# Which rows SP and ACT fetch, and when: a four-part graph network on one core

## The chip, the cores and the metric

The kernel runs on one core of a Trainium2 chip. Times are device microseconds (us) of whole executions. The engines named below are TensorE (PE), VectorE (DVE), ScalarE (ACT), GpSimd (POOL) and SyncE (SP); each has its own instruction stream, and they meet only through semaphores. SP, ACT and POOL issue DMAs. A gather with row numbers in memory (an indirect DMA) is issued by POOL; SP and ACT issue plain transfers, whose address may come from a register.

## The reference

12,500 nodes with 64 features, 200,000 edges sorted by target node (`dst`). Four graph layers follow each other; each normalises x, applies relu and adds its result to x.

```python
h = relu(layernorm(x)); x = x + L0(h)   # attention: k, q, v per node type, 4 heads, weights per edge type
h = relu(layernorm(x)); x = x + L1(h)   # gated: edge score, softmax per target, max and mean of neighbours
h = relu(layernorm(x)); x = x + L2(h)   # polynomial of edge weights, from sum(h) of one end
h = relu(layernorm(x)); x = x + L3(h)   # three convolutions over edges:
# conv(h, W, b): m = concat(h[dst], h[src], edge_attr) @ W + b; segment_sum(m, dst)
# segment softmax, sum and max run over the edges with the same dst
```

What costs most is `h[src]`, one table row per edge, in five places: attention, gated, and three convolutions.

## The kernel before

**Layout.** The sorted edges are cut into 128 runs, one per partition, of J = 1564 edges. A step handles C = 23 edge columns of all partitions; NC = 68 steps make a pass. Sums over equal targets are running scans along the columns; a carry from partition to partition is mended afterwards through a "fixed row".

**Sequence.** `first_phase` (tables), `attention_edges_phase` (pass 1), `carry_phase`, `attention_end_phase`, `gated_edges_phase` (pass 2), `carry_phase`, `gated_end_phase`, and `conv_layer` three times (passes 3 to 5). Each phase opens a block of its own, in which every engine gets its list of instructions; at a block's end all engines drain and meet in a barrier. After `first_phase`, `attention_end_phase`, `gated_end_phase` and each `conv_layer` stands `clear_semaphores` (line 203): a block of its own in which SP clears the layer's semaphores, one instruction each (line 210).

**Gathering the source rows.** In `gather_columns` (line 905) POOL issues, for step c and each of its columns, one indirect DMA of 128 rows (line 912) into buffer c % ring, and before a step it waits until that buffer has been used (`ring` is 3 in attention and gated, 2 in conv). An *aided* step (`aided`, line 875) has one column less: its last column is brought by 128 one-row transfers in `fetch_rows` (line 889), in chunks of 16 rows, each with one load of 16 byte offsets into registers (line 896) and 16 transfers (line 901). `ATT_SHARE = (2, 5)` makes 25 of the first 64 steps aided in attention and gated, `CONV_SHARE = (3, 4)` makes 48 aided in each conv layer.

**Who fetches, and when.** In attention and gated SP fetches all 128 rows, half of them one iteration earlier than the other half. In conv SP fetches 80 and ACT 48, all for step c+2 in iteration c, once the copy of step c (`s_in`) has freed the buffer. These stand in order with SP's other work: in attention a load of q rows, then rows, then the wait for ACT's copy (`s_copied`) of the step before and its store; in gated rows, the wait for this step's copy, its store (line 1518); in conv the edge attributes (layer 0 alone, line 2125), some rows, the store (line 2148), the remaining rows.

**A gated step** (lines 1561 to 1615): DVE waits for the gathered rows and, if the step is aided, for the one-row transfers; it starts with line 1571, multiplies the rows by the exponentials at line 1603 (which signals `s_wtd`: the buffer is free), and scans. ACT then copies the results to the store buffer (to line 1539) and SP stores them. An attention step is alike: line 1055 is the first that uses gathered rows, ACT's exponentials begin at line 1006, and line 985 stores the last step (983 the others). In a conv step ACT copies the gathered rows (line 2190), DVE scans (line 2334), ACT copies the result (line 2195), SP stores it.

Of the kernel before, what the change touches and what calls it, by code (L numbers as in the profile page):

```python
# [28 lines left out]
P = 128  # L29
N = 12500  # L30
E = 200000
D = 64
H = 4
# [48 lines left out]
ATT_SHARE = (2, 5)  # L82
CONV_SHARE = (3, 4)
SP_ROWS = 80
# [200 lines left out]
def first_phase(nc, ctx, g, a):  # L285
# [3 lines left out]
    s_listed = sem("listed")  # L289
# [89 lines left out]
    with ExitStack() as inner:  # L379
# [8 lines left out]
        block = inner.enter_context(nc.Block())  # L388
# [277 lines left out]
        def _(dve):  # L666
# [205 lines left out]
            v.tensor_copy(g.a2row[:, :], ps_w[:, 260:260 + D])  # L872
# [55 lines left out]
def attention_edges_phase(nc, ctx, g):  # L928
# [27 lines left out]
    with nc.psum_tensor("ae_keep", [P, HF * C1], F32) as keep, nc.psum_tensor("ae_work", [P, HF * C1], F32) as work, \  # L956
            nc.psum_tensor("ae_prob", [P, C, H], F32) as prob_t, nc.Block() as block:
# [3 lines left out]

        @block.gpsimd
        def _(pool):

            pool.indirect_dma_start(out=mix[:, :, :].rearrange("p f j -> p (f j)")[:, 0:D], out_offset=None, in_=g.q_tab,
                                    in_offset=bass.IndirectOffsetOnAxis(ap=g.first[:, 0:1].bitcast(U32), axis=0))\
# [4 lines left out]
        def _(sp):  # L971
            for c in range(NC):
                wait(sp, s_qt, c)
                sp.dma_start(qin, q_rows[:, c * C:c * C + C, :]).then_inc(s_qin, 16)
                for later in (0, 1):
                    if aided(c + later, ATT_SHARE):
                        wait(sp, s_wtd, c + later - 2)
                        chunks = range(0, P // LOADS // 2) if later else range(P // LOADS // 2 if c else 0, P // LOADS)
                        fetch_rows(nc, sp, mybir.EngineType.SP, g.lists[:, 0, :], g.tab0, c + later, chunks,
                                   kvr[(c + later) % 3], s_side[side_of(c + later, ATT_SHARE)[0]])  # L980
# [8 lines left out]
        def _(act):  # L989
            def take(c):  # L990
# [28 lines left out]
        def _(dve):  # L1019
            v = nc.vector  # L1020
# [199 lines left out]
def attention_end_phase(nc, ctx, g, agg):  # L1220
# [34 lines left out]
    with ExitStack() as inner:  # L1255
# [4 lines left out]
        block = inner.enter_context(nc.Block())  # L1260
# [173 lines left out]


# [28 lines left out]
def gated_edges_phase(nc, ctx, g):  # L1464
# [26 lines left out]
    with nc.psum_tensor("ge_pen", [P, HF * C1], F32) as pen_flat, nc.psum_tensor("ge_decay", [P, HF * C1], F32) as decay_flat, \  # L1491
            nc.psum_tensor("ge_small", [P, 2, C], F32) as few, nc.Block() as block:  # L1492
# [4 lines left out]

        @block.gpsimd
        def _(pool):
            pool.indirect_dma_start(out=fv, out_offset=None, in_=g.s_tab,  # L1500
                                    in_offset=bass.IndirectOffsetOnAxis(ap=g.first[:, 0:1].bitcast(U32), axis=0))\
                .then_inc(s_first, 16)
            gather_columns(pool, g.tab1, g.src, rin, s_gath, s_wtd, ATT_SHARE)

        @block.sync
        def _(sp):
            sp.wait_ge(g.s_scattered, 16 * T)
            sp.dma_start(g.spread[:, :], g.s_start[0:EP, :].rearrange("(p j) a -> p (j a)", p=P)).then_inc(s_sin, 16)
            for c in range(NC):
                for later in (1, 2) if c else (0, 1, 2):  # L1510
                    if aided(c + later, ATT_SHARE):
                        wait(sp, s_wtd, c + later - 2)
                        half = P // LOADS // 2
                        chunks = range(0, half) if later == 2 else range(half if c else 0, 2 * half)
                        fetch_rows(nc, sp, mybir.EngineType.SP, g.lists[:, 1, :], g.tab1, c + later, chunks,
                                   rin[(c + later) % 3], s_side[side_of(c + later, ATT_SHARE)[0]])
                wait(sp, s_copied, c + 1)
                sp.dma_start(dest[:, c * C:c * C + C, 0:R1], out).then_inc(s_st, 16)
# [3 lines left out]
        def _(act):  # L1522
            act.wait_ge(s_init, 1)
            for c in range(NC):
# [8 lines left out]
                nc.scalar.activation(wts, args[:, 1, 1:C1], ACT.Exp).then_inc(s_den, 1)  # L1533

# [7 lines left out]
        def _(dve):  # L1542
            v = nc.vector
# [14 lines left out]
            for c in range(NC):  # L1558
# [7 lines left out]
                dve.wait_ge(s_gath[c % 3], gathered(c, ATT_SHARE, 3))  # L1566
                if aided(c, ATT_SHARE):
                    slot, full = side_of(c, ATT_SHARE)
# [473 lines left out]
def conv_layer(nc, ctx, g, a, k, out_rows):  # L2042
# [9 lines left out]
    s_gath = [pool_sem(g, f"gathered{b}") for b in range(2)]  # L2052
    s_side = [sem(f"side{n}") for n in range(4)]
    s_row = pool_sem(g, "fixed_rows")
# [10 lines left out]
    rin, ea, hd = ([None] * 2 for _ in range(3))  # L2065
    for b in range(2):
# [21 lines left out]
    with ExitStack() as inner:  # L2088
# [7 lines left out]
        def side_rows(eng, engine, c, chunks):  # L2096

            if aided(c, CONV_SHARE):
                fetch_rows(nc, eng, engine, g.lists[:, 2, :], g.tab3, c, chunks, rin[c % 2],
                           s_side[side_of(c, CONV_SHARE)[0]])  # L2100

        @block.gpsimd
        def _(pool):
            gather_columns(pool, g.tab3, g.src, rin, s_gath, s_in, CONV_SHARE)
# [16 lines left out]
        def _(sp):  # L2121
# [17 lines left out]
            early, late = range(0, SP_ROWS // LOADS // 2), range(SP_ROWS // LOADS // 2, SP_ROWS // LOADS)  # L2139
            for c in range(2):  # L2140
                side_rows(sp, mybir.EngineType.SP, c, range(0, SP_ROWS // LOADS))
# [32 lines left out]
        def _(act):  # L2174
            def take(c):
# [7 lines left out]
                act.wait_ge(s_gath[b], gathered(c, CONV_SHARE, 2))  # L2183
                if aided(c, CONV_SHARE):
                    slot, full = side_of(c, CONV_SHARE)
# [4 lines left out]
                nc.scalar.copy(chain[:, 0:D, 1:C1], rin[b].rearrange("p j f -> p f j")).then_inc(s_in, 1)  # L2190
# [25 lines left out]
            of_act = range(SP_ROWS // LOADS, P // LOADS)  # L2216
            scale(0)
            for c in range(2):
                side_rows(act, mybir.EngineType.Activation, c, of_act)
            for c in range(NC):  # L2220
# [10 lines left out]
                if len(of_act):  # L2231
                    act.wait_ge(s_in, c + 1)
                    side_rows(act, mybir.EngineType.Activation, c + 2, of_act)
# [129 lines left out]
def graph_layers(nc, a, out):  # L2363
    with ExitStack() as whole:
# [3 lines left out]
        with ExitStack() as ctx:  # L2368
            first_phase(nc, ctx, g, a)
            clear_semaphores(nc)  # L2370
        with ExitStack() as ctx:
            last = attention_edges_phase(nc, ctx, g)[:, C - 1, :]
# [4 lines left out]
            attention_end_phase(nc, ctx, g, agg)  # L2377
            clear_semaphores(nc)
        with ExitStack() as ctx:
            last = gated_edges_phase(nc, ctx, g)[:, C - 1, :]  # L2380
# [31 lines left out]
```

## Time and profile before

| | us |
|---|---|
| median of 3 runs (11754.08 to 11767.4) | 11756.29 |
| the profiled execution | 11757.73 |
| its span | 11755.6 |
| busy in the span: POOL | 8127.3 |
| busy: DVE | 4012.2 |
| busy: ACT | 3490.3 |
| busy: PE | 1335.8 |

The profiled execution is one run with the hardware profiler; its span goes from the first to the last instruction. Busy time counts instructions on an engine; register, branch, semaphore and DMA-issuing instructions are not counted, so SP has none, and ACT's and SP's work on one-row transfers appears only in the timeline (as SPq and ACTq, where consecutive instructions of one kind are merged into one line). A busy POOL is the time of its indirect DMA instructions, not of the transfers.

### The profile page before, as it was taken

The page shows a single profiled execution, that of the slowest core. Times are in us where ns is not written, and L with a number is a line of the kernel's source. Part 1 is how long each engine was busy: PE and PEld are TensorE (multiplying, and loading weights), DVE is VectorE, ACT ScalarE, POOL GpSimd, SP SyncE. Part 2 cuts the span into 40 slices and gives each one's busy share as a digit, 9 for nine tenths or more (in the row PEclk, how much of TensorE's full clock was granted, in tenths as well). Part 3 has the DMA queues.
Part 4 walks back from the last instruction along what each step waited for, and adds up shares of the span by engine and source line. Part 5 has one row for each costly group of instructions (what it writes and reads, how often), then busy time and mean ns, then how long its engine had stood idle before and what let it go on. Part 6 is the DMA issues. An engine that isn't in the chain of part 4 may idle for free. (4 is left out here: it accounts for less than half of the span.)

```text
span 11755.6 us, 88443 instructions
## 1 busy us (share of the span) xinstructions
PE 1335.8 (11%) x6735; PEld 1000.0 (9%) x6735; DVE 4012.2 (34%) x5478; ACT 3490.3 (30%) x4561; POOL 8127.3 (69%) x8534
## 2 busy tenths in 40 slices
PE   6100000030000000496111000200000010000001
PEld 4100000020000000374000000200000010000001
DVE  3365555645555555696111111111111101111111
ACT  3333333312222222375333222223222212332221
POOL 5777777677777776401777777677777767777776
PEclk8555555555555555798555555555555555555555
DMA  9333333323333333000222222222222212222222
GB/s 348 129 112 108 108 108 111 105 39 102 110 110 107 113 107 81 13 1 23 67 65 66 65 68 62 62 51 56 53 56 56 53 50 51 56 53 56 56 53 50
DMA packets 448676, 922.38 MB, mean 78 GB/s; under 512 B 211206, under 2 KB 241837, under 8 KB 432952
## 3 DMA queue, kind: packets, MB, share of 16 engines
q0 software_dynamic: 272736, 378.88, 14.7%
q1 hardware_dynamic: 157672, 535.74, 12.5%
q14 instruction: 573, 4.69, 0.1%
q10 hardware_dynamic: 17648, 2.29, 0.1%
q8 instruction: 47, 0.77, 0.0%
HBM read 456.45 MB, written 459.77 MB: 78 GB/s over the span
## 5 line engine op out<-in xcount | busy, mean ns | idle before, releaser
L912 POOL DMA_INDIRECT arena<-tab,src x6087 | 5746.2, 944 | 2631.0 <-issue 1890.5
L2334 DVE TENSOR_TENSOR_SCAN arena<-cv_keep,arena 128x768 f32<-128x768 f32 (+1 forms) x476 | 751.9, 1627 | 5040.6 <-ACT arena L2190 5040.6
L912 POOL DMA_INDIRECT arena<-tab,spread x1539 | 1453.1, 944 | 469.3 <-issue 469.0
L2179 ACT COPY cv_keep<-keep 128x736 f32<-128x736 f32 x204 | 166.0, 814 | 2707.6 <-issue 2707.6
L2195 ACT COPY arena<-arena 128x1472 f32<-128x1472 f32 (+1 forms) x204 | 588.2, 2883 | 551.6 <-DVE arena L2334 551.6
L2190 ACT COPY arena<-arena 128x1472 f32<-128x1472 f32 x204 | 545.2, 2673 | 666.4 <-DMA arena<-tab,src 430.0
L1147 PE MATMUL e_t<-ident,arena 128*68 128x128 f32 (+1 forms) x2 | 0.8, 396 | 4037.2 <-PEq L1492 2046.4
L2258 PE MATMUL cv_t<-ident,arena 128*81 128x128 f32 (+1 forms) x294 | 137.9, 469 | 2616.8 <-ACT arena L2202 1722.9
L1147 PEld LDWEIGHTS e_t<-ident,arena 128*68 128x68 f32 (+1 forms) x2 | 0.3, 132 | 4037.6 <-issue 4037.6
L2272 PE MATMUL cv_t<-ident,arena 128*64 128x128 f32 (+1 forms) x3 | 1.3, 426 | 2975.7 <-ACT arena L2195 2975.7
L1835 PE MATMUL po_u<-arena,Hn 128*128 128x448 bf16 x1564 | 300.9, 354 | 279.9 <-DVE Hn L1942 279.9
L1952 DVE TENSOR_SCALAR arena<-arena 128x448 bf16<-128x448 f16 x1252 | 322.9, 327 | 21.1 <-PE po_u L1835 20.9
L1006 ACT ACTIVATE ae_prob<-arena 128x92 f32<-128x92 f32 x68 | 17.1, 251 | 977.0 <-DVE arena L1077 977.0
L1835 PE MATMUL po_u<-arena 128*128 128x448 bf16 x1564 | 298.9, 353 | 0.7 <-DVE arena L1952 0.7
L998 ACT ACTIVATE ae_work<-arena 128x768 f32<-128x768 f32 x136 | 208.7, 1534 | 300.4 <-DVE arena L1095 300.4
L1531 ACT ACTIVATE ge_decay<-arena 128x768 f32<-128x768 f32 x68 | 56.2, 827 | 776.1 <-DVE arena L1593 776.1
L2258 PEld LDWEIGHTS cv_t<-ident,arena 128*81 128x81 f32 (+1 forms) x294 | 53.9, 183 | 2653.8 <-ACT arena L2202 1736.0
L1571 DVE TENSOR_TENSOR arena<-arena,ge_small 128x23 f32<-128x23 f32 x68 | 13.3, 195 | 776.7 <-DMA arena<-tab,src 454.9
L1092 DVE TENSOR_TENSOR_SCAN arena<-ae_work,arena 128x768 f32<-128x768 f32 x136 | 238.9, 1756 | 115.2 <-ACT ae_work L998 108.1
L1083 DVE TENSOR_TENSOR arena<-arena,ae_prob 128x1472 f32<-128x1472 f32 x68 | 259.9, 3822 | 21.6 <-ACT ae_prob L1006 21.2
L1047 DVE TENSOR_TENSOR_SCAN ae_work<-ae_keep,arena 128x768 f32<-128x768 f32 x136 | 240.1, 1766 | 78.5 <-ACT arena L995 76.1
L1575 DVE TENSOR_TENSOR arena<-arena,ge_small 128x1472 f32<-128x1472 f32 x68 | 259.1, 3810 | 0.2 <-issue 0.2
(373 smaller groups left out, 6810.2 us busy)
## 6 DMA issues: line engine op xcount, KB each, us to landing
arena<-tab SPq DMA_DIRECT2D x11520, 0.2 KB
arena<-tab ACTq DMA_DIRECT2D x6912, 0.2 KB
rows<-arena SPq DMA_DIRECT2D x68, 1506.5 KB, 5.6
rows3b<-arena SPq DMA_DIRECT2D x136, 736.0 KB
arena<-tab,src POOLq DMA_INDIRECT x6087
rows<-arena SPq DMA_DIRECT2D x68, 920.0 KB
rows<-arena SPq DMA_DIRECT2D x68, 828.0 KB, 4.5
arena<-tab SPq DMA_DIRECT2D x3200, 0.5 KB
```

What stands on the lines that cost most here:

```text
L912: pool.indirect_dma_start(out=rows[b][:, j, :], out_offset=None, in_=table, in_offset=bass.IndirectOffsetOnAxis(ap=idx[:, at:at + 1].bitca ...
L998: return nc.scalar.activation(works.rearrange("p (h d) j -> p h d j", h=HH), args[:, 0, :, h0:h0 + HH].rearrange("p j h -> p h j").unsquee ...
L1047: v.tensor_tensor_scan(out=work[:, :], data0=keep[:, :], data1=qts[:, x * HF * C1:(x + 1) * HF * C1], initial=0.0, op0=ALU.mult, op1=ALU.a ...
L1083: v.tensor_tensor(mix[:, :, 1:C1].rearrange("p (h d) j -> p j h d", h=H), kv[:, :, D:2 * D].rearrange("p j (h d) -> p j h d", h=H), prob.u ...
L1092: ins = v.tensor_tensor_scan(out=part, data0=work[:, :], data1=part, initial=0.0, op0=ALU.mult, op1=ALU.add)
L1575: v.tensor_tensor(peak[:, :, 1:C1].rearrange("p f j -> p j f"), r[:, :, D:2 * D], pre.unsqueeze(2).to_broadcast([P, C, D]), ALU.mult).then ...
L1835: ins = nc.tensor.matmul(ps_u[:, x, 0:half], wide[c % 2][:, x * P:x * P + P, j], ring[:, n % RING, :], start=(n == 0), stop=(n == J - 1))
L1952: v.tensor_scalar(ring[:, n % RING, :], iota_hi, hi[:, n:n + 1], None, ALU.is_equal).then_inc(s_hot, 1)
L2190: nc.scalar.copy(chain[:, 0:D, 1:C1], rin[b].rearrange("p j f -> p f j")).then_inc(s_in, 1)
L2195: nc.scalar.copy(rows.rearrange("p j f -> p f j"), chain[:, :, 1:C1]).then_inc(s_copied, 1)
L2258: nc.tensor.transpose(ps_t[b][0:K_Z, 0:P], hd[b][:, 0:K_Z], g.ident[:, :]).then_inc(s_tr, 1)
L2334: ins = v.tensor_tensor_scan(out=part, data0=keep[:, 0:(f1 - f0) * C1], data1=part, initial=0.0, op0=ALU.mult, op1=ALU.add)
```

## The change

Four things are done at once.

- *Shares and plan.* Attention and gated get a share of 1 in 2 (32 aided steps each, the odd ones), conv layer 0 gets 2 in 3 (42), layers 1 and 2 keep 3 in 4. A new function, `rows_plan`, assigns the chunks (step, chunk) of one engine to that engine's iterations: in order, at the latest in iteration step + `closes`, and earlier, from step + `opens`, if an even spread over the 64 steps has reached them. In attention and gated SP takes 96 rows and ACT 32; in conv 80 and 48 as before.
- *Buffers.* Conv gathers into three buffers instead of two.
- *Blocks.* `first_phase` and `attention_edges_phase` share a block, and so do `attention_end_phase` and `gated_edges_phase`. The first of each pair returns `over`, a list of waits with which every engine but PE begins the second. The clear that stood before the edge phase stands behind it now, in front of `carry_phase`.
- *Clears.* SP clears runs of consecutive semaphore numbers with one instruction each.

```diff
-ATT_SHARE = (2, 5)
-CONV_SHARE = (3, 4)
-SP_ROWS = 80
+ATT_SHARE = (1, 2)
+GATED_SHARE = (1, 2)
+CONV_SHARE = ((2, 3), (3, 4), (3, 4))
+SP_EDGE = 96
+SP_CONV = 80
 # clear_semaphores
-            for handle in LAYER:
-                sp.sem_clear(handle)
+            numbers = sorted(handle.num for handle in LAYER)
+            first = numbers[0]
+            for n, after in zip(numbers, numbers[1:] + [None]):
+                if after != n + 1:
+                    sp.sem_clear(range(first, n + 1))
+                    first = after
 # first_phase: s_over is signalled by DVE's last copy
+    def over(eng):
+        eng.wait_ge(s_over, 1)
+        eng.wait_ge(s_zero, 16 * (9 + BLANKS // 2))
+        eng.wait_ge(s_qdone, 16 * (FULL + 1))
+        for b in range(2):
+            eng.wait_ge(s_st[b], 16 * ((TWOS + 1 - b) // 2))
+        eng.wait_ge(s_scat, 16 * T)
+    return over
+def rows_plan(share, first, stop, opens, closes):
+    jobs = [(c, k) for c in range(LISTED) if aided(c, share) for k in range(first // LOADS, stop // LOADS)]
+    plan = [[] for _ in range(NC)]
+    at = 0
+    for i in range(NC):
+        while at < len(jobs) and (jobs[at][0] + closes <= i or
+                                  jobs[at][0] + opens <= i and at * LISTED < (i + 1) * len(jobs)):
+            plan[i].append(jobs[at])
+            at += 1
+    return plan
 # attention_edges_phase
+        of_sp = rows_plan(ATT_SHARE, 0, SP_EDGE, -1, 0)
+        of_act = rows_plan(ATT_SHARE, SP_EDGE, P, -3, -2)
...
                 sp.dma_start(qin, q_rows[:, c * C:c * C + C, :]).then_inc(s_qin, 16)
-                for later in (0, 1):
-                    if aided(c + later, ATT_SHARE):
-                        wait(sp, s_wtd, c + later - 2)
...
+                for x, k in of_sp[c]:
+                    wait(sp, s_wtd, x - 2)
+                    side_rows(sp, mybir.EngineType.SP, x, k)
                 if c:
                     wait(sp, s_copied, c)
...
                 nc.scalar.copy(out[:, :, 0:D].rearrange("p j f -> p f j"), mix[:, :, 1:C1]).then_inc(s_copied, 1)
+                for x, k in of_act[c]:
+                    wait(act, s_wtd, x - 2)
+                    side_rows(act, mybir.EngineType.Activation, x, k)
 # attention_end_phase
+    def over(eng):
+        eng.wait_ge(s_gate, GROUPS)
+        for b in range(2):
+            eng.wait_ge(s_tab[b], 16 * ((GROUPS + 1 - b) // 2))
+        eng.wait_ge(s_tabd, 16)
+    return over
 # gated_edges_phase
+        of_sp = rows_plan(GATED_SHARE, 0, SP_EDGE, -2, -1)
+        of_act = rows_plan(GATED_SHARE, SP_EDGE, P, -2, -1)
...
             for c in range(NC):
-                for later in (1, 2) if c else (0, 1, 2):
-                    if aided(c + later, ATT_SHARE):
-                        wait(sp, s_wtd, c + later - 2)
-                        half = P // LOADS // 2
-                        chunks = range(0, half) if later == 2 else range(half if c else 0, 2 * half)
...
+                for x, k in of_sp[c]:
+                    wait(sp, s_wtd, x - 2)
+                    side_rows(sp, mybir.EngineType.SP, x, k)
                 wait(sp, s_copied, c + 1)
                 sp.dma_start(dest[:, c * C:c * C + C, 0:R1], out).then_inc(s_st, 16)
...
                 nc.scalar.activation(wts, args[:, 1, 1:C1], ACT.Exp).then_inc(s_den, 1)
+                for x, k in of_act[c]:
+                    wait(act, s_wtd, x - 2)
+                    side_rows(act, mybir.EngineType.Activation, x, k)
                 act.wait_ge(s_rows, c + 1)
 # conv_layer: three buffers rin, share = CONV_SHARE[k]
+        of_sp = rows_plan(share, 0, SP_CONV, -3, -2)
+        of_act = rows_plan(share, SP_CONV, P, -3, -2)
...
             for c in range(NC):
-                wait(sp, s_in, c + 1)
-                if k == 0 and c + 2 < NC:
+                wait(sp, s_in, c + 1 if c else 0)
+                if k == 0 and c + 2 < NC and c:
                     load_attrs(c + 2)
-                side_rows(sp, mybir.EngineType.SP, c + 2, early)
+                half = (len(of_sp[c]) + 1) // 2 if c else len(of_sp[c])
+                for x, part in of_sp[c][:half]:
+                    side_rows(sp, mybir.EngineType.SP, x, part)
...
                 wait(sp, s_copied, c + 1)
                 sp.dma_start(dest[:, c * C:c * C + C, :], rows).then_inc(s_st, 16)
-                side_rows(sp, mybir.EngineType.SP, c + 2, late)
+                for x, part in of_sp[c][half:]:
+                    side_rows(sp, mybir.EngineType.SP, x, part)
 # ACT: of_act[0] before its first step, of_act[c] at the end of step c (c > 0), as before
```

## Rows read from the trace of the kernel before

**Rows 1.** Busy us (count) by stage: PE, PEld, DVE, ACT, POOL; clock, DMA share, GB/s.

```profile
391.00:2313.00 1922.00, 0.00 (x0) 0.00 (x0) 1136.43 (x1544) 655.91 (x538) 1452.96 (x1539) 0.50 0.36 110
2634.00:4559.00 1925.00, 0.00 (x0) 0.00 (x0) 1078.97 (x1207) 516.62 (x606) 1455.66 (x1540) 0.50 0.37 108
5520.00:7475.00 1955.00, 96.74 (x293) 61.37 (x293) 285.04 (x205) 580.91 (x629) 1430.17 (x1516) 0.50 0.24 66
7630.00:9538.00 1908.00, 76.69 (x294) 64.56 (x293) 228.52 (x138) 497.24 (x659) 1430.20 (x1516) 0.50 0.21 54
```

**Rows 2.** Waits of POOL: line, what it waited for, us in all, times, longest.

```profile
POOL arena L912 <- issue: 2359.5, 7599, 2.9
...
POOL arena L912 <- ACT arena L2190: 57.4, 23, 3.9
```

**Rows 3.** Timeline of SP in the gated stretch (start, us, count).

```profile
4219.74 0.37 SPq L1518 DMA_DIRECT2D rows<-arena  x1
4223.64 26.19 SPq L901 DMA_DIRECT2D arena<-tab  x64
```

**Rows 4.** Timeline of the attention stretch, last step.

```profile
2314.79 0.24 DVE L1055 COPY arena<-ae_work 128x32 f32<-128x32 f32 x1 [6.18 <-DMA arena<-tab,spread]
...
2322.03 0.25 ACT L1006 ACTIVATE ae_prob<-arena 128x92 f32<-128x92 f32 x1 [12.31 <-DVE arena L1077]
...
2335.09 0.34 SPq L985 DMA_DIRECT2D rows<-arena  x1
```

**Rows 5.** Timeline of SP and ACT in conv layer 0, four steps.

```profile
6310.20 18.70 SPq L901 DMA_DIRECT2D arena<-tab  x48
...
6336.34 12.48 SPq L901 DMA_DIRECT2D arena<-tab  x32
...
6374.10 12.05 SPq L901 DMA_DIRECT2D arena<-tab  x32
...
6276.40 2.67 ACT L2190 COPY arena<-arena 128x1472 f32<-128x1472 f32 x1
...
6331.12 2.67 ACT L2190 COPY arena<-arena 128x1472 f32<-128x1472 f32 x1
...
6339.49 20.82 ACTq L901 DMA_DIRECT2D arena<-tab  x48
...
6393.32 2.67 ACT L2190 COPY arena<-arena 128x1472 f32<-128x1472 f32 x1
```

**Rows 6.** Timeline of the gated stretch, step 54, an aided one.

```profile
4191.23 5.29 SPq L901 DMA_DIRECT2D arena<-tab  x16
...
4197.70 0.20 DVE L1571 TENSOR_TENSOR arena<-arena,ge_small 128x23 f32<-128x23 f32 x1 [13.14 <-DMA arena<-tab]
...
4206.62 3.80 DVE L1603 TENSOR_TENSOR arena<-arena,ge_small 128x1472 f32<-128x1472 f32 x1
```

**Rows 7.** Waits of DVE in the gated stretch.

```profile
DVE arena L1571 <- DMA arena<-tab: 289.5, 23, 13.7
```

**Rows 8.** Timeline of POOL: first instructions of three phases (start, us, [idle before]).

```profile
389.77 0.98 POOL L965 DMA_INDIRECT arena<-q_tab,first  x1 [13.70 <-PEq L957]
...
2349.69 0.97 POOL L1267 DMA_INDIRECT arena<-rows,end_i  x1 [2.55 <-POOLq L1121]
...
2633.40 0.98 POOL L1500 DMA_INDIRECT arena<-s_tab,first  x1 [13.54 <-PEq L1492]
```

**Rows 9.** Timeline: DVE's last in the first phase, SP's in the attention's end.

```profile
348.27 0.21 DVE L872 COPY a2row<-fp_samples 128x64 f32<-128x64 f32 x1
...
2542.60 1.21 SPq L1283 DMA_DIRECT2D s_tab<-small  x1
```

**Rows 10.** DMA issues: the scatters, count, us from issue to landing.

```profile
s_start<-small,start_i POOLq DMA_INDIRECT x196, 2.2
```

**Rows 11.** Line 210 in two stretches: count, ns min/median/max, first and last start.

```profile
L210 SPq EVENT_SEMAPHORE_RANGE_CLEAR  x59: 25/25/30, 5515.5 to 5518.8; - x59
...
L210 SPq EVENT_SEMAPHORE_RANGE_CLEAR  x32: 25/28/35, 7627.2 to 7628.9; - x32
```

More of the change, by code:

```diff
@@ L282, in norm_root, with first_phase @@
     nc.scalar.activation(bufs[2], bufs[2], ACT.Sqrt).then_inc(s_root, 1)
-def first_phase(nc, ctx, g, a):
+def first_phase(nc, ctx, g, a, block):
     sem = lambda n: new_sem(nc, ctx, "fp_" + n)
-    s_listed = sem("listed")
+    s_listed, s_over = sem("listed"), sem("over")
     s_pad, s_din, s_xin, s_ein, s_w, s_wlate, s_wconv, s_zero = map(sem, (
@@ L387, in first_phase @@
         ps_w = ps_s
-        block = inner.enter_context(nc.Block())
         @block.sync
@@ L926, in to_psum, with attention_edges_phase @@
     ins.then_inc(s_flags, 1)
-def attention_edges_phase(nc, ctx, g):
+def attention_edges_phase(nc, ctx, g, block, over):
     sem = lambda n: new_sem(nc, ctx, "ae_" + n)
@@ L960, in attention_edges_phase, with side_rows @@
         works = work[:, :].rearrange("p (f j) -> p f j", j=C1)
+        of_sp = rows_plan(ATT_SHARE, 0, SP_EDGE, -1, 0)
+        of_act = rows_plan(ATT_SHARE, SP_EDGE, P, -3, -2)
+        def side_rows(eng, engine, c, k):
+            fetch_rows(nc, eng, engine, g.lists[:, 0, :], g.tab0, c, range(k, k + 1), kvr[c % 3],
+                       s_side[side_of(c, ATT_SHARE)[0]])
         @block.gpsimd
         def _(pool):
+            over(pool)
             pool.indirect_dma_start(out=mix[:, :, :].rearrange("p f j -> p (f j)")[:, 0:D], out_offset=None, in_=g.q_tab,
@@ L971, in _ @@
         def _(sp):
+            over(sp)
             for c in range(NC):
@@ L989, in _ @@
         def _(act):
+            over(act)
             def take(c):
@@ L1218, in _, with attention_end_phase @@
             v.tensor_tensor(row[:, 0:count], row[:, 0:count], back_s[:, 0:count], ALU.add).then_inc(s_put, 1)
-def attention_end_phase(nc, ctx, g, agg):
+def attention_end_phase(nc, ctx, g, agg, block):
     sem = lambda n: new_sem(nc, ctx, "ao_" + n)
@@ L1461, in turn_pairs, with gated_edges_phase @@
         multiply(y).then_inc(s_mm, 1)
-def gated_edges_phase(nc, ctx, g):
+def gated_edges_phase(nc, ctx, g, block, over):
     sem = lambda n: new_sem(nc, ctx, "ge_" + n)
@@ L1496, in gated_edges_phase, with side_rows @@
         pre, prob = few[:, 0, :], few[:, 1, :]
+        of_sp = rows_plan(GATED_SHARE, 0, SP_EDGE, -2, -1)
+        of_act = rows_plan(GATED_SHARE, SP_EDGE, P, -2, -1)
+        def side_rows(eng, engine, c, k):
+            fetch_rows(nc, eng, engine, g.lists[:, 1, :], g.tab1, c, range(k, k + 1), rin[c % 3],
+                       s_side[side_of(c, GATED_SHARE)[0]])
         @block.gpsimd
         def _(pool):
+            over(pool)
             pool.indirect_dma_start(out=fv, out_offset=None, in_=g.s_tab,
@@ L1502, in _ @@
                 .then_inc(s_first, 16)
-            gather_columns(pool, g.tab1, g.src, rin, s_gath, s_wtd, ATT_SHARE)
+            gather_columns(pool, g.tab1, g.src, rin, s_gath, s_wtd, GATED_SHARE)
         @block.sync
         def _(sp):
+            over(sp)
             sp.wait_ge(g.s_scattered, 16 * T)
@@ L1522, in _ @@
         def _(act):
+            over(act)
             act.wait_ge(s_init, 1)
@@ L1542, in _ @@
         def _(dve):
+            over(dve)
             v = nc.vector
@@ L1565, in _ @@
                 dve.wait_ge(s_flags, c + 1)
-                dve.wait_ge(s_gath[c % 3], gathered(c, ATT_SHARE, 3))
-                if aided(c, ATT_SHARE):
-                    slot, full = side_of(c, ATT_SHARE)
+                dve.wait_ge(s_gath[c % 3], gathered(c, GATED_SHARE, 3))
+                if aided(c, GATED_SHARE):
+                    slot, full = side_of(c, GATED_SHARE)
                     dve.wait_ge(s_side[slot], full)
@@ L2051, in conv_layer @@
     s_ea = [sem(f"attrs{b}") for b in range(2)]
-    s_gath = [pool_sem(g, f"gathered{b}") for b in range(2)]
+    s_gath = [pool_sem(g, f"gathered{b}") for b in range(3)]
     s_side = [sem(f"side{n}") for n in range(4)]
+    share = CONV_SHARE[k]
     s_row = pool_sem(g, "fixed_rows")
@@ L2064, in conv_layer @@
     at = 0
-    rin, ea, hd = ([None] * 2 for _ in range(3))
-    for b in range(2):
+    rin = [None] * 3
+    ea, hd = ([None] * 2 for _ in range(2))
+    for b in range(3):
         rin[b], at = view(g, at, C, D)
@@ L2094, in conv_layer, with side_rows @@
         block = inner.enter_context(nc.Block())
[L2096 to L2100, printed above, removed]
+        of_sp = rows_plan(share, 0, SP_CONV, -3, -2)
+        of_act = rows_plan(share, SP_CONV, P, -3, -2)
+        def side_rows(eng, engine, c, k):
+            wait(eng, s_in, c - 2)
+            fetch_rows(nc, eng, engine, g.lists[:, 2, :], g.tab3, c, range(k, k + 1), rin[c % 3],
+                       s_side[side_of(c, share)[0]])
         @block.gpsimd
         def _(pool):
-            gather_columns(pool, g.tab3, g.src, rin, s_gath, s_in, CONV_SHARE)
+            gather_columns(pool, g.tab3, g.src, rin, s_gath, s_in, share)
             fix = bass.IndirectOffsetOnAxis(ap=g.fix[:, 0:1].bitcast(U32), axis=0)
@@ L2138, in _ @@
                     load_attrs(c)
-            early, late = range(0, SP_ROWS // LOADS // 2), range(SP_ROWS // LOADS // 2, SP_ROWS // LOADS)
-            for c in range(2):
-                side_rows(sp, mybir.EngineType.SP, c, range(0, SP_ROWS // LOADS))
             for c in range(NC):
-                wait(sp, s_in, c + 1)
-                if k == 0 and c + 2 < NC:
+                wait(sp, s_in, c + 1 if c else 0)
+                if k == 0 and c + 2 < NC and c:
                     load_attrs(c + 2)
-                side_rows(sp, mybir.EngineType.SP, c + 2, early)
+                half = (len(of_sp[c]) + 1) // 2 if c else len(of_sp[c])
+                for x, part in of_sp[c][:half]:
+                    side_rows(sp, mybir.EngineType.SP, x, part)
+                if k == 0 and not c:
+                    wait(sp, s_in, 1)
+                    load_attrs(2)
                 wait(sp, s_copied, c + 1)
                 sp.dma_start(dest[:, c * C:c * C + C, :], rows).then_inc(s_st, 16)
-                side_rows(sp, mybir.EngineType.SP, c + 2, late)
+                for x, part in of_sp[c][half:]:
+                    side_rows(sp, mybir.EngineType.SP, x, part)
             n_out = 0
@@ L2182, in take @@
                     act.wait_ge(s_chained, c)
-                act.wait_ge(s_gath[b], gathered(c, CONV_SHARE, 2))
-                if aided(c, CONV_SHARE):
-                    slot, full = side_of(c, CONV_SHARE)
+                act.wait_ge(s_gath[c % 3], gathered(c, share, 3))
+                if aided(c, share):
+                    slot, full = side_of(c, share)
                     act.wait_ge(s_side[slot], full)
@@ L2189, in take @@
                     nc.scalar.copy(chain[:, D:R3, 1:C1], ea[b].rearrange("p j f -> p f j"))
-                nc.scalar.copy(chain[:, 0:D, 1:C1], rin[b].rearrange("p j f -> p f j")).then_inc(s_in, 1)
+                nc.scalar.copy(chain[:, 0:D, 1:C1], rin[c % 3].rearrange("p j f -> p f j")).then_inc(s_in, 1)
             def give(c):
@@ L2214, in copy_z @@
                 nc.scalar.copy(z[:, t, :], ps_o[b][:, 0:D]).then_inc(s_z, 1)
-            of_act = range(SP_ROWS // LOADS, P // LOADS)
             scale(0)
-            for c in range(2):
-                side_rows(act, mybir.EngineType.Activation, c, of_act)
+            for x, part in of_act[0]:
+                side_rows(act, mybir.EngineType.Activation, x, part)
             for c in range(NC):
@@ L2230, in _ @@
                 give(c)
-                if len(of_act):
-                    act.wait_ge(s_in, c + 1)
-                    side_rows(act, mybir.EngineType.Activation, c + 2, of_act)
+                if c:
+                    for x, part in of_act[c]:
+                        side_rows(act, mybir.EngineType.Activation, x, part)
             def relu(q):
@@ L2368, in graph_layers @@
         with ExitStack() as ctx:
-            first_phase(nc, ctx, g, a)
+            with nc.Block() as block:
+                over = first_phase(nc, ctx, g, a, block)
+                last = attention_edges_phase(nc, ctx, g, block, over)[:, C - 1, :]
             clear_semaphores(nc)
         with ExitStack() as ctx:
-            last = attention_edges_phase(nc, ctx, g)[:, C - 1, :]
             agg, _ = view(g, 0, T, R0)
@@ L2376, in graph_layers @@
                              + [(D + H + h, D + h, 1) for h in range(H)]))
-            attention_end_phase(nc, ctx, g, agg)
+            with nc.Block() as block:
+                over = attention_end_phase(nc, ctx, g, agg, block)
+                last = gated_edges_phase(nc, ctx, g, block, over)[:, C - 1, :]
             clear_semaphores(nc)
         with ExitStack() as ctx:
-            last = gated_edges_phase(nc, ctx, g)[:, C - 1, :]
             agg, _ = view(g, 0, T, R1)
```

13 lines of the change are left out of this document (4 added, 9 removed).

## The prediction

> **What bounds the kernel now.** I read the busy times by stage first, then POOL's waits, then the timeline at the places that the diff touches. Five stretches gather the edges' source rows: attention, gated, and three conv layers, of which the last two are alike; 1922 + 1925 + 1955 + 2 x 1908 = 9618 of the 11755.6 us [rows 1]. In each, POOL issues 1516 to 1539 column gathers and is busy 73 to 76% of the time, and no other engine passes 60%. Divide the attention stretch by its gathers: 1922 / 1539 = 1.249 us each, 0.944 of it busy; nearly all idle time in front of a gather is "issue", 2359.5 us over 7599 of them, 0.31 each [rows 1, 2]. So a stretch lasts 1.249 us times its gathers, plus stalls. Conv layer 0 has 1955 - 1516 x 1.249 = 61.5 us of stalls, layers 1 and 2 14.5 each, attention none, gated 1.5. Of layer 0's, 23 waits for ACT's copy of the gathered rows (line 2190) make 57.4 us [rows 2]; less their normal 0.3 each that is 50.5.
>
> A column that is "aided" isn't gathered by POOL: 128 one-row transfers bring it, issued by SP and ACT. A step of 23 gathers lasts 28.7 us, an aided one of 22 lasts 27.5.
>
> **The change part by part.**
>
> *Attention rows.* Aided steps go from 25 (2 in 5) to 32 (every odd step): 7 gathers less, -8.7 us, if the rows come in time. SP now issues 96 of the 128, 48 in the iteration before and 48 in that of the step. A store and register loads in front of the first row take 3.9 us and 64 rows 26.2 [rows 3], so 48 take 19.6: an iteration of 24 us with its q load, against 28.1 per step. A step runs 20.3 us from its gathered data to the store of its result [rows 4]. From one such store over the rows, their landing (1.2) and the aided step that uses them to its store: 45 us in two steps, against 45 x 1.249 = 56.2. ACT's 32 rows, by its 48 in 20.8 us [rows 5] 13.9, stand behind the copy that ends at 2335.1; ACT is next needed 28.7 us after its exponential at 2322.0 [rows 4], so 1.7 us are left. If ACT misses that, DVE's step is later and POOL, with three buffers, isn't. I take -8.7; the other end is 15 us worse, if POOL gets here the 14.5 us that it loses in conv layer 1, where ACT issues rows too.
>
> *Gated rows.* The same share, -8.7 us of gathers, but look at the plan. Jobs are handed out in order, a job for step x in iteration x-1 at the latest. In x-2 the evenness test compares 6n x 64 with 2n x 192: equal, not smaller. So all six chunks, 96 rows, fall into the even iteration x-1 and none into the odd one. SP's order is: the rows of x, then the wait for step x-1's copy and its store; and the iteration before ended with the wait for step x-2's copy and its store. So the rows of an aided step are never begun before the previous aided step is stored, and the step can't begin before they land. That closes a loop, and each link is in the trace. Step 54's store 4219.74, next first row 4223.64: 3.9. 64 rows in 26.19, so 96 in 39.3 [rows 3]. From the end of the last row's issue (4196.52) to the first DVE instruction, which a landing row releases: 1.2. From that (4197.70) to the store: 22.0 [rows 3, 6]. Together 66.4 us for two steps that POOL needs 56.2 for. The chain was harmless before, because a column's rows were split over two iterations and only two columns came in five steps; even so 23 of DVE's steps waited for rows, 289.5 us in all [rows 7]. Three buffers put the excess off and don't remove it: POOL will wait for the product at line 1603 of the step three back.
>
> The stretch then ends so. POOL starts at 2620.2 (below). Its first load, 45 gathers and a landing (1.3 + 56.2 + 1.7) start step 1 at 2679.4, and its store is at 2701.4. 31 loops of 66.4 put step 63's store at 4759.8. Line 1603 ends 9.3 before the store (4210.42 and 4219.74 [rows 3, 6]), so POOL may gather step 66 from 4750.5, and 66 and 67 are unaided: 57.5. Last gather at 4808, against 4559 now: +249 us, the new start included. Ends: at SP's quickest pace in conv layer 0 (48 rows in 18.7 [rows 5]) the loop is 64.5, -59 us; if ACT's new rows or later stores cost it 2 us each time, +62.
>
> *Shared blocks.* After the last scatter of the first phase POOL idles 13.7 us, after that of the attention's end phase 13.5 [rows 8]. The other engines issued their last work long before, by 349 and 2544 [rows 9], so in one block POOL waits in the first case for its own scatter alone, which lands 2.2 us after its issue [rows 10], 1.2 after its end. I start it at 377.6 instead of 389.8 (-12.2), and in the second place, where the gathers need no scatter, at 2620.2 instead of 2633.4 (counted above). If what POOL does in those 13 us is owed all the same, each is 0. Each clear moves behind an edge phase, into a block of its own: one block change more there. Between the carry and the next phase POOL idles 2.55 us for one [rows 8], 1.2 of them a landing: 1.3, with the ranges 1.6, twice: +3.2.
>
> *Range clears.* 59 clears take 3.3 us in front of layer 0, 32 take 1.8 at the end of each layer [rows 11], every one between two barriers. With some 0.3 left: -3.0 and three times -1.6, -7.8. Ends 0 and -9.
>
> *Conv.* Layer 0 goes from 48 to 42 aided: +7.5. Its stalls are SP's. Four steps take 116.9 us (line 2190 from 6276.40 to 6393.32), POOL needs 89 x 1.249 = 111.2; two aided columns begin 37.8 us apart, and the end of the third one's rows (6328.9) releases the copy at 6331.1, which the next column waits for [rows 5]. With 2 in 3, a column leaves the cycle: 116.9 - 37.8 = 79.1 us for three steps, and POOL needs 83.7. So POOL bounds again and the 50.5 us go. The plan gives every column to iteration x-2, as before; the third buffer adds slack. Net -43.0; if all stalls stayed, +7.5. In layers 1 and 2 shares and places stay: 0. Their first iteration now brings two columns before the first store, but 70 us of rows stand against 84 until step 2 is gathered.
>
> Sum: -12.2 - 8.7 + 249 + 3.2 - 7.8 - 43.0 = +180.5. The profiled execution took 11757.7 us (the span and 2.1 around it), so 11938; the median of the runs is 1.4 lower: 11937.
>
> **The rivals.**
>
> *POOL stays the bound in the gated stretch* (the faster side). Then it gains the 8.7 and 13.2 instead of losing 249: 11667. For it: three buffers, ACT taking a quarter of the rows, and hardly a POOL stall there with 25 columns. Against: the loop's links are dependencies, each of them measured. It decides at a loop of 56.2 us: SP would have to issue 96 rows in 29.1 us, 0.30 each with register loads, and the trace shows 0.41.
>
> The Trainium skill, DMA: Bandwidth & Descriptors, section Issuing engines are not separate DMA queues, speaks for this rival: starting DMAs on several engines saves only the sequencer's time, usually small beside the DMA. By it the rows would cost little more than a landing and the time would be this rival's. The trace disagrees for one-row transfers: 64 of them hold SP for 26.19 us [rows 3].
>
> *Layer 0 keeps its stalls:* 11937 + 50 = 11987. For: 79.1 against 83.7 is a slim 4.6 us. Against: a column less in the cycle, a buffer more.
>
> *Drains owed, ACT's issues felt:* the 12.2 and 13.2 don't come and attention loses 15: 11977.
>
> **How the numbers follow.** Forecast 0.72, POOL-bound gated stretch 0.10, layer 0 unrelieved 0.09, owed drains 0.09. The forecast's own range is 11880 to 12000; with the two rivals above it 11865 to 12005, which leaves out the faster one and the tails. A measurement of this kernel can tell 0.2% (24 us) from no change; only the faster rival, or mixtures with it, lies below 11780. Slower 0.87, same 0.02, faster 0.11.
>
> **What would show it.** In the gated stretch: about 2185 us for 1532 gathers, POOL waiting some 10 us for DVE's product once in two steps, DVE waiting for one-row transfers in about 31 steps, SP's 96 rows in one run. The attention stretch should be 1913 us without POOL waits; layer 0 near 1912 with only its short stalls left; POOL's idle time at the two joined borders about 1.5 and 0.3 us. If the gated stretch is about 1915 us, the loop is wrong and the forecast with it.

## The result, and the profile after

| | before | after |
|---|---|---|
| median of 4 runs each, us | 11756.44 (11754.08 to 11767.4) | 11925.72 (11924.62 to 11935.05) |
| ratio, 95% interval | | 1.0144 [1.0131, 1.0157] |
| span of the profiled execution, us | 11755.6 | 11933.2 |
| predicted, us | | 11937 (11865 to 12005) |

The kernel became slower, by 169 us, for the reason given: the gated stretch lost 272 us, everything else together gained some 94 us in the profiled execution. That execution, at 11935.05, is the slowest of the four.

The stretches first: busy us (count) of PE, PEld, DVE, ACT and POOL, then clock, DMA share and GB/s, kernel after, to be laid beside [rows 1].

```profile
381.00:2297.00 1916.00, 0.00 (x0) 0.00 (x0) 1137.28 (x1544) 655.59 (x538) 1448.53 (x1533) 0.50 0.36 110
2604.00:4801.00 2197.00, 0.00 (x0) 0.00 (x0) 1065.73 (x1192) 507.45 (x594) 1450.12 (x1533) 0.50 0.31 94
5780.00:7683.00 1903.00, 97.13 (x294) 61.45 (x294) 285.77 (x206) 580.44 (x630) 1437.85 (x1522) 0.50 0.24 67
7836.00:9731.00 1895.00, 76.96 (x294) 64.85 (x294) 229.05 (x140) 497.32 (x661) 1432.09 (x1516) 0.50 0.20 54
9882.00:11777.00 1895.00, 76.83 (x294) 64.73 (x294) 228.62 (x139) 497.03 (x659) 1432.06 (x1516) 0.50 0.20 54
```

The gated stretch has seven gathers fewer than before and no engine has more counted work in it, and yet it is 272 us longer: time in which the engines wait. (DVE and ACT show a little less here only because their last two steps fall behind the window.) Who waits is in the waits of POOL over the whole span (line, what for, us in all, times, longest). ACT's copy, 57.4 us in [rows 2], is gone; DVE's product of the gated steps is new.

```profile
POOL arena L940 <- issue: 2315.4, 7587, 0.4
POOL arena L940 <- DVE arena L1662: 287.0, 28, 11.1
```

28 waits, one in each even step from step 12 on. The next three views show one turn of the loop. SP's timeline (start, us, line, count): a store, 96 one-row transfers, the next store, and the store of the aided step itself.

```profile
4151.68 0.36 SPq L1572 DMA_DIRECT2D rows<-arena  x1
4155.14 39.26 SPq L929 DMA_DIRECT2D arena<-tab  x96
4194.45 0.38 SPq L1572 DMA_DIRECT2D rows<-arena  x1
4217.76 0.36 SPq L1572 DMA_DIRECT2D rows<-arena  x1
```

DVE's timeline (in brackets the idle time before an instruction and what ended it): the aided step can start 1.36 us after the last of those rows is issued (4194.40), and the product that frees a buffer (line 1662, before: 1603) ends at 4208.44. From one aided step's store to the next: 3.46 + 39.26 + 1.36 + 22.0 = 66.1 us.

```profile
4195.76 0.20 DVE L1630 TENSOR_TENSOR arena<-arena,ge_small 128x23 f32<-128x23 f32 x1 [26.57 <-DMA arena<-tab]
4204.65 3.79 DVE L1662 TENSOR_TENSOR arena<-arena,ge_small 128x1472 f32<-128x1472 f32 x1
```

POOL's timeline: two gathers that waited for that product, 66.09 us apart. In this time POOL has 45 gathers to issue, 56.2 us of work.

```profile
4142.62 0.94 POOL L940 DMA_INDIRECT arena<-tab,src  x1 [10.68 <-DVE arena L1662]
4208.71 0.94 POOL L940 DMA_INDIRECT arena<-tab,src  x1 [10.09 <-DVE arena L1662]
```

DVE's waits in the gated stretch, against 289.5 us in 23 times in [rows 7]:

```profile
DVE arena L1630 <- DMA arena<-tab: 832.7, 31, 27.6
```

The borders, by POOL's timeline ([rows 8] had 13.70 and 13.54 of idle time at the first two):

```profile
380.33 0.98 POOL L1002 DMA_INDIRECT arena<-q_tab,first  x1 [2.33 <-issue]
2603.43 0.98 POOL L1557 DMA_INDIRECT arena<-s_tab,first  x1 [0.30 <-issue]
4850.98 0.94 POOL L1168 DMA_INDIRECT arena<-rows,fix  x1 [50.17 <-SPq L1161]
```

The third line is the carry phase behind the gated stretch; POOL idles 50.17 us there, against 29.77 in the kernel before:

```profile
4588.67 0.94 POOL L1128 DMA_INDIRECT arena<-rows,fix  x1 [29.77 <-SPq L1121]
```

Both borders have closed. The clears are 31 instructions instead of 245 (line, count, ns, first and last start):

```profile
L215 SPq EVENT_SEMAPHORE_RANGE_CLEAR  x31: 30/35/107, 2322.5 to 11932.9; - x31
```

### The profile page after: what moved, and what is told of

Same layout as the page of the kernel before. It is cut to its first block and busy times, and to the rows that moved or that the text cites. A ratio compares the mean times of both kernels' runs of the same rounds, so it can differ in the third digit from the quotient of the medians.

```text
span 11933.2 us, 90414 instructions
## 1 busy us (share of the span) xinstructions
PE 1336.4 (11%) x6735; PEld 998.9 (8%) x6735; DVE 4013.5 (34%) x5478; ACT 3489.2 (29%) x4561; POOL 8130.2 (68%) x8526
## 5 line engine op out<-in xcount | busy, mean ns | idle before, releaser
L1586 ACT ACTIVATE ge_decay<-arena 128x768 f32<-128x768 f32 x68 | 56.2, 827 | 1029.8 <-DVE arena L1652 1029.8
```

## The experiments

Stretches are measured from the start of the first gather to the end of the last. Ratios are to executions of the kernel before beside each experiment (medians 11759.77 us, for the last three 11761.21).

**Where the loop is cut: SP's 96 rows in two halves.** The kernel after, with three chunks of a gated column in the iteration two before the step and three in the one before it. Shares, buffers, blocks and clears stay.

```diff
-of_sp = rows_plan(GATED_SHARE, 0, SP_EDGE, -2, -1)
+of_sp = [[] for _ in range(NC)]
+for x in range(LISTED):
+    for k in range(SP_EDGE // LOADS if aided(x, GATED_SHARE) else 0):
+        of_sp[max(x - (2 if k < 3 else 1), 0)].append((x, k))
```

> The changed kernel, but in the gated stretch SP's 96 rows of an aided step are cut in two: three chunks in the iteration two before the step, three in the one before it. Theory (loop over store, 96 rows, landing, aided step, store: 66.1 us for two steps): the rows behind one store are 48, the loop about 47 us, so POOL bounds with 56.2: no waits of POOL for DVE's product, stretch about 1918 us instead of 2196, its tail to the carry back from 50 to 30 us, whole kernel about 11627. Rival (ACT's 32 new rows, which stand in front of the copies in every even step, hold the chain): nothing changes, stretch about 2196. Rival (rows of two queues land late): rows still end DVE's waits, stretch over 2100.

Measured: 11627.74 us (11625.01 to 11628.92), 0.9888 [0.9871, 0.9904] of before. The gated stretch took 1915.1 us. SP's timeline now has a store every 23 to 32 us and 48 rows between two:

```profile
4205.05 0.37 SPq L1575 DMA_DIRECT2D rows<-arena  x1
4208.89 19.10 SPq L929 DMA_DIRECT2D arena<-tab  x48
4236.89 0.38 SPq L1575 DMA_DIRECT2D rows<-arena  x1
4240.93 19.14 SPq L929 DMA_DIRECT2D arena<-tab  x48
4260.12 0.38 SPq L1575 DMA_DIRECT2D rows<-arena  x1
```

POOL's waits over the span no longer have a row for DVE's product:

```profile
POOL arena L940 <- issue: 2323.2, 7615, 0.3
POOL arena L1168 <- SPq L1161: 59.3, 2, 30.5
```

The same rows, issued by the same engine in the same number, cost nothing when they stand on both sides of a store. 298 us of the median hang on this one choice of place; in the profiled executions 281 of them lie in the stretch and 20 in the longest wait in front of the carry phase, which is 30.5 again. ACT's rows stand where they stood, so the rival that they hold the chain falls.

**The dose: 80 rows for SP, 48 for ACT.** The kernel after, still with all of SP's chunks in one iteration.

```diff
-of_sp = rows_plan(GATED_SHARE, 0, SP_EDGE, -2, -1)
-of_act = rows_plan(GATED_SHARE, SP_EDGE, P, -2, -1)
+of_sp = rows_plan(GATED_SHARE, 0, 80, -2, -1)
+of_act = rows_plan(GATED_SHARE, 80, P, -2, -1)
```

> The changed kernel, but in the gated stretch SP fetches 80 rows of an aided step and ACT 48, all still in one iteration. Theory (loop): the row term falls by 16 of 96, 39.3 to 32.7, the loop from 66.1 to 59.5, still over 56.2: POOL waits about 3 to 4 us once in two steps instead of 10, stretch 2196 - 31 x 6.6 = about 1991. Rival (ACT's rows in front of the copies): ACT has 16 rows more, 6.2 us, in every second step, so the stretch is longer, about 2380.

Measured, one execution: 11718.3 us, gated stretch 1988.6. SP's timeline, POOL's waits in the span, and POOL's timeline over one turn:

```profile
4061.36 0.36 SPq L1572 DMA_DIRECT2D rows<-arena  x1
4065.50 32.88 SPq L929 DMA_DIRECT2D arena<-tab  x80
4098.43 0.38 SPq L1572 DMA_DIRECT2D rows<-arena  x1
```

```profile
POOL arena L940 <- DVE arena L1662: 79.4, 21, 5.2
```

```profile
4052.30 0.94 POOL L940 DMA_INDIRECT arena<-tab,src  x1 [3.51 <-DVE arena L1662]
4112.61 0.94 POOL L940 DMA_INDIRECT arena<-tab,src  x1 [4.43 <-DVE arena L1662]
```

16 rows less take 6.38 us from SP's block (39.26 to 32.88), and the turn shrinks by the same amount, from 66.5 to 60.3; the stretch loses 207.5 us. ACT issues half as many rows again, so if ACT's issues were what holds the step, this kernel would have become slower.

**The block one iteration earlier.** The kernel after, with SP's 96 rows of a step due two iterations ahead.

```diff
-of_sp = rows_plan(GATED_SHARE, 0, SP_EDGE, -2, -1)
+of_sp = rows_plan(GATED_SHARE, 0, SP_EDGE, -3, -2)
```

> The changed kernel, but in the gated stretch SP's 96 rows of an aided step stand in one run one iteration earlier, two before the step. Theory (order behind SP's stores): no gain. The store of the step in between now stands behind the rows, and DVE's scan of the next step waits for its landing: 3.5 + 39.3 + 0.4 + 5.6 + 17.6 = 66.4 us for two steps, up to 4 more because that step is the one with ACT's rows; stretch 2200 to 2330, DVE's waits for the store (line 1644) instead of for rows. Rival (only the rows' lateness matters): rows come a step sooner, stretch about 1918.

Measured, one execution: 12009.01 us, gated stretch 2280.7: worse still, though the rows are now there in time. DVE's waits in the stretch (no row for one-row transfers is left among them), POOL's, and SP's timeline:

```profile
DVE arena L1644 <- DMA rows<-arena: 638.5, 64, 21.2
```

```profile
POOL arena L940 <- DVE arena L1662: 374.3, 28, 14.1
```

```profile
4112.94 0.36 SPq L1572 DMA_DIRECT2D rows<-arena  x1
4116.30 39.83 SPq L929 DMA_DIRECT2D arena<-tab  x96
4156.18 0.38 SPq L1572 DMA_DIRECT2D rows<-arena  x1
```

DVE now waits for a store that stands behind the block. The loop has only changed the way by which it closes: still one store, 96 rows, the next store, with a step of DVE between. Lateness of the rows alone, which an earlier start would cure, isn't the cause; the block between two stores is.

**Blocks and clears alone.** The kernel before, with the two joined blocks and the range clears.

```diff
 # graph_layers: one nc.Block() for each of the two pairs of phases,
 # the first returns `over`, with which the second begins;
 # clear_semaphores clears ranges. Shares, plans, buffers as before.
```

> The kernel before with the shared blocks and the range clears alone. Theory: the borders and clears are independent of the rest: first border -9.4, second -14, clears and moved blocks about -6, together about -29, whole kernel about 11727; gated without stalls; the short stalls inside the conv layers (12 to 15 us each, once in about 111 gathers) stay, because they belong to the two buffers. Rival (the short stalls come from where the program's code lies, which the blocks move): they go here too, whole kernel about 11690.

Measured: 11730.03 us (11727.76 to 11734.72), 0.9976 [0.9966, 0.9985]. The borders by POOL's timeline, and POOL's waits for ACT's copy, which stay:

```profile
378.03 0.98 POOL L980 DMA_INDIRECT arena<-q_tab,first  x1 [2.33 <-issue]
2609.26 0.98 POOL L1528 DMA_INDIRECT arena<-s_tab,first  x1 [0.31 <-issue]
```

```profile
POOL arena L926 <- issue: 2358.5, 7600, 2.7
POOL arena L926 <- ACT arena L2221: 57.3, 23, 3.7
```

The kernel before that ran beside it had 11759.77, so this is 30 us less: the 13 us at each border don't come back elsewhere, nothing is owed. The short stalls in the conv layers stay (the longest wait is 2.7), so the rival that they come from where the code lies falls too.

**Conv's third buffer alone**, in the kernel before:

```diff
-    s_gath = [pool_sem(g, f"gathered{b}") for b in range(2)]
+    s_gath = [pool_sem(g, f"gathered{b}") for b in range(3)]
...
-                act.wait_ge(s_gath[b], gathered(c, CONV_SHARE, 2))
+                act.wait_ge(s_gath[c % 3], gathered(c, CONV_SHARE, 3))
...
```

> The kernel before with a third gather buffer in the conv layers alone; shares, places and order of the rows as before. Theory (the short stalls inside the conv layers belong to two buffers; layer 0's long ones to SP's cycle of three columns): short stalls go in all three layers (-12, -14, -14); SP's cycle of 116.9 us for four steps stays, so layer 0 still drifts 5.7 us in four steps, but POOL stalls 20 steps later, and of the 50 us some 20 to 30 are left; whole kernel about 11690. Rival (the buffer alone cures layer 0): its stretch is 1516 x 1.249 = 1894, whole about 11667. Rival (the short stalls have another cause): they stay, and the whole is about 11730.

Measured: 11703.09 us (11700.08 to 11711.07), 0.995 [0.9933, 0.9966]. Layer 0 took 1924.9 us, layers 1 and 2 1894.7 each. POOL's waits in layer 0 (without the first gather's, at the block's start):

```profile
POOL arena L912 <- issue: 457.8, 1499, 0.4
POOL arena L912 <- ACT arena L2191: 34.8, 16, 4.3
```

Layer 0 keeps 34.8 - 16 x 0.3 = 30 of the 50.5 us above the normal 0.3: the buffer puts SP's excess off, from step 24 to step 44, and doesn't remove it. That is the upper end of what was expected, and the whole is 13 us over it. What it does remove are the short stalls, in all three layers. The waits of POOL in layer 1 show them, in the kernel before:

```profile
POOL arena L912 <- issue: 477.7, 1515, 2.9
```

and here:

```profile
POOL arena L912 <- issue: 462.3, 1515, 0.3
```

The same number of gathers with the same releaser, 15.4 us less, and the longest falls from 2.9 to 0.3. These are 13 stalls of 0.3 to 2.6 us in each of layers 1 and 2 of the kernel before, at the second or third gather of every fifth step. In layer 0 there are 9; at the other four places POOL has just waited for the copy.

**Layer 0's share alone**, in the kernel before, two buffers:

```diff
+    share = (2, 3) if k == 0 else CONV_SHARE
...
-                act.wait_ge(s_gath[b], gathered(c, CONV_SHARE, 2))
+                act.wait_ge(s_gath[b], gathered(c, share, 2))
...
```

> The kernel before with two aided steps in three instead of three in four in conv layer 0 alone, two buffers as before. Theory (SP's cycle): a column less, 79.1 us for three steps against POOL's 83.7, so the long stalls go without a third buffer: layer 0 from 1955 to 1522 x 1.249 = 1901 and its short stalls of about 12, 1913; layers 1 and 2 keep theirs; whole about 11716. Rival (the third buffer was what cured layer 0): the waits for the copy of the gathered rows stay, layer 0 at 1950 or more, whole about 11760.

Measured: 11725.86 us (11722.82 to 11728.76), 0.997 [0.9959, 0.9982]. Layer 0 took 1920.1 us, 34.5 less, though with 6 gathers more; no wait for ACT's copy is left in it:

```profile
POOL arena L912 <- issue: 484.1, 1521, 2.9
```

12 short stalls of 20.0 us together stay (about 12 us were expected), and layers 1 and 2 keep 15.0 and 14.4. So the share removes the long waits, the buffer the short ones, and neither does both.

**What the experiments point to: 2 in 3 aided in attention and gated, no block over 64 rows after the first iteration.** The kernel after, with SP's five chunks (80 rows) of a column over two iterations, three and two or one and four, and ACT's three as two and one or one and two.

```diff
-ATT_SHARE = (1, 2)
-GATED_SHARE = (1, 2)
-SP_EDGE = 96
+ATT_SHARE = (2, 3)
+GATED_SHARE = (2, 3)
+SP_EDGE = 80
...
+def two_iterations(share, first, stop, back, split):
...
+            n = split[c % 3 == 2]
+            for k in ks:
+                plan[max(c - back + (k - ks[0] >= n), 0)].append((c, k))
...
-        of_sp = rows_plan(GATED_SHARE, 0, SP_EDGE, -2, -1)
+        of_sp = two_iterations(GATED_SHARE, 0, SP_EDGE, 2, (3, 1))
...
```

> The changed kernel with two aided steps in three in attention and gated, too, SP 80 and ACT 48 rows, each step's rows cut over two iterations so that SP issues at most four chunks between two stores and ACT at most two in a step. Theory (POOL bounds as long as each loop is under its steps' gathers): 1522 gathers in each, about 1901 us, 12 less than the split version in both, whole about 11604. Rival (ACT's rows in every gated step in front of the copies: 25.5 us from first instruction to copy and about 1 to the next step, 26 to 28 us against 27.9): the gated stretch is bound by DVE and ACT and takes up to 1960.

Measured: 11600.57 us (11599.28 to 11601.47), 0.9863 [0.9847, 0.988] of before, faster than both kernels. Attention and gated in the windows (columns as above):

```profile
381.00:2282.00 1901.00, 0.00 (x0) 0.00 (x0) 1137.48 (x1544) 655.80 (x538) 1436.95 (x1522) 0.50 0.38 111
2591.00:4495.00 1904.00, 0.00 (x0) 0.00 (x0) 1080.62 (x1207) 515.16 (x603) 1438.68 (x1523) 0.50 0.39 110
```

1522 gathers x 1.249 = 1901.0 and stretches of 1901.1 and 1902.6: with 42 aided steps POOL is the bound to within 2 us. More rows in all weren't the trouble, and the rival (1960 us in the gated stretch) falls.

## Why the prediction was right

The spans of the two profiled executions, term by term (measured: first gather to last, and the time between the stretches):

| term | predicted, us | measured, us |
|---|---|---|
| first border | -12.2 | -9.4 |
| attention, 1922.1 to 1915.2 | -8.7 | -6.9 |
| attention's end, second border, one block change | -11.6 | -13.7 |
| gated, 1924.2 to 2196.1 | +262.2 | +271.9 |
| gated's end to layer 0 | -1.4 | +19.1 |
| layer 0, 1954.6 to 1901.8 | -43.0 | -52.8 |
| layers 1 and 2, 3814.9 to 3788.6 | 0 | -26.3 |
| ends of the layers | -4.8 | -4.2 |
| sum (of the unrounded terms) | +180.5 | +177.6 |

*The gated loop: right, link by link.* Stores of odd steps lie 66.53 us apart in the mean over 31 turns, predicted 66.4. The first and the last of them on SP's timeline:

```profile
2690.22 0.37 SPq L1572 DMA_DIRECT2D rows<-arena  x1
4752.69 0.36 SPq L1572 DMA_DIRECT2D rows<-arena  x1
```

The links of the turn shown above are 3.5, 39.3, 1.4 and 22.0, predicted 3.9, 39.3, 1.2 and 22.0; 31 steps wait for rows, as said. That it is a loop through SP's order and not a shortage of SP's, ACT's or POOL's time is shown from three sides: the dose (-6.38 us of rows, -6.2 us a turn), the cut (no loop, no loss), and the earlier block (the loop goes by the store). The +9.7 beyond the term: step 1's store came 86.8 us after POOL's start, where I had added up 81.2, and 31 x 0.13 = 4.

*The rival of a POOL-bound gated stretch* is refuted for this plan and true for the split one: 1915.1 us, what that rival gave. The sentence of the Trainium skill behind it (DMA: Bandwidth & Descriptors, section Issuing engines are not separate DMA queues: the sequencer's time is usually small beside the DMA) isn't borne out for a block of one-row transfers; 96 of them hold SP for 39.26 us, while DVE starts on the last one 1.36 us after its issue, and those 39.26 us are the largest link of the loop.

*Borders: right.* Idle times of 2.33 and 0.30 us, predicted 1.5 and 0.3; the first moved the first gather by only 9.4 us, because the first phase ended 2 us later in this execution and the wait is 0.8 longer than added up. Blocks and clears alone give -30 us (11759.77 to 11730.03), predicted from the same terms -12.2 - 13.2 + 3.2 - 7.8 = -30: the rival of owed drains falls.

*Attention: right.* No wait of POOL appears there, so ACT's 32 rows cost nothing, and the share gives 7 gathers: 8.8 us in the kernel with split rows, 6.9 in this execution, whose gathers lie 1.250 us apart instead of 1.249.

*Layer 0: right in its cause.* The 50.5 us went by SP losing a column in three steps, as the share alone shows; the rival that they stay is refuted. The term is 9.8 too small because the short stalls inside the layer went too.

*Where it was wrong, in two steps whose errors nearly cancel.* First, "In layers 1 and 2 shares and places stay: 0" is a step that failed: I had seen 14.5 us of stalls in each and let them stand, although the third buffer is a change in those layers too. It removes them: -26.3 in two layers, as the kernel with the buffer alone shows; in layer 0 it is worth 18 us beside the new share (1920.1 with the share alone, 1901.8 with both). Second, the end of the gated stretch: I ended the loss with POOL's last gather and let the rest follow as before. But after a loop DVE is behind, not POOL. The last gather ends at 4800.8, and DVE's timeline shows steps 66 and 67 only beginning then:

```profile
4799.44 0.20 DVE L1630 TENSOR_TENSOR arena<-arena,ge_small 128x23 f32<-128x23 f32 x1 [6.48 <-ACT ge_small L1583]
4822.37 0.20 DVE L1630 TENSOR_TENSOR arena<-arena,ge_small 128x23 f32<-128x23 f32 x1 [6.46 <-ACT ge_small L1583]
```

The last store follows at 4844.3, and POOL's first gather of the carry phase waits 50.17 us instead of 29.77: +20.4. In the kernel with split rows that wait is 30.5. That the sum is within 3 us is luck: +20.5, -26.3, -9.8 and the +9.7 of the loop nearly cancel, and the profiled execution is 9 us above the median, against which the forecast is 11 us too high. Of the loop's own 271.9 the reasoning had 262.2; that was no luck.

*Open.* What the short stalls are. They go with the third buffer and with nothing else that was tried, and they come every fifth step whether 3 in 4 steps are aided or 2 in 3. What POOL waits for there the profile doesn't name ("issue"), and no kernel here separates it.

## What to carry to other kernels

Where an in-order queue holds both a block of issues and a store or wait of the consumer, add up the closed way (store, block, landing, consumer's step, store) and set it against the time that the producers need for the same steps; a spare buffer only puts off an excess, and splitting the block over the store removes it without taking away any work. When a plan spreads jobs by a comparison, work out by hand what it does where both sides are equal: here a tie put all six chunks into one iteration. And after a loss by a loop, look at which engine is behind at the stretch's end, since its backlog is paid once more in front of the next phase.

## What the runs showed of the hardware that I had not expected

- The two borders cost POOL 13.5 to 13.7 us of idle time, of which 2.33 and 0.30 are left when the phases share a block, and none of it has to be paid later. Each border held two changes of block with a clear between them; a single change behind one scatter leaves 2.55 [rows 8]. At the first border the clears begin 9.7 us after POOL's last scatter ends (376.07) and take 2.5, and POOL goes on 1.5 us behind them:

```profile
L210 SPq EVENT_SEMAPHORE_RANGE_CLEAR  x42: 25/30/49, 385.8 to 388.3; - x42
```

  Why those 9.7 us are so long, behind a run of scatters and with all other engines long done, no run separates.
- With two gather buffers POOL lost 0.3 to 2.6 us at every fifth step of a conv layer, in waits that name no engine, 11.6 to 15.3 us a layer of the kernel before; with three none of these stalls is left. Both held in all three layers.
- The same gathers lay 1.249 us apart in most of the profiled executions and 1.250 in two, those of the kernel after and of conv's third buffer alone, each 7 to 9 us above the next of its kernel. POOL's rows show it as longer instructions (in a conv layer 944.7 ns in the mean instead of 943.5), 9 us over 7600 gathers; what makes them longer no run shows.
